# Four layers of cross attention on one core: layer 2's score products moved to the GELU, the first unit's odd maxima copied to f16 by ScalarE, the mask count cut in eight

## What is computed

```python
# layers 0, 1, 3 (with their own norms, biases and residuals)
scores = einsum('bhqd,bhkd->bhqk', q, k) * scale        # 16 heads, 100 x 1444
out    = einsum('bhqk,bhkd->bhqd', softmax(scores), v)
# layer 1 also has a mask of 100 x 1444 (all zero in the inputs)
# layer 2
sim    = softmax(where(causal, Q @ K.T / 8 ** 0.5, -1e9))
att_h  = layer_norm(sim @ V + q)
out    = gelu(att_h @ W1.T + b1, approximate=False) @ W2.T + b2 + att_h
```

## Time and profile before

| | us |
|---|---|
| median of three runs | 1051.69 |
| the profiled execution | 1052.03 |
| its span, first to last instruction | 1050.2 |
| stages -3 to -1 (ahead of the first exponential) | 76.7 |
| stages 0 to 5, each | 36.7 to 39.0 |
| stages 6 to 11, each | 35.1 to 35.4 |
| stage 12 (layer 2's attention alone) | 41.9 |
| stages 13 to 19 (attention and feed-forward), each | 50.4 to 53.1 |
| stage 20 (feed-forward alone) | 41.6 |
| stages 21, 22 | 34.6, 29.0 |

### The profile page before, as it was taken

One profiled execution on the slowest core, in us unless ns is written; L12 is line 12 of the kernel. 1 busy time (PEld: TensorE's weight loads), 2 busy tenths in 40 slices (PEclk: granted clock), 3 DMA queues, 4 the chain that ended last, 5 costly groups with the idle time before them and its releaser, 6 DMA issues.

```text
span 1050.2 us, 43883 instructions
## 1 busy us (share of the span) xinstructions
PE 947.4 (90%) x18826; PEld 570.9 (54%) x18826; DVE 839.8 (80%) x1804; ACT 717.6 (68%) x1621; POOL 372.3 (35%) x404
## 2 busy tenths in 40 slices
PE   1889999999989999999998979898979898989996
PEld 1346556656656665666564545555645464555552
DVE  7888988889788888889987777777878787869851
ACT  1147777777767777777776676667666676767786
POOL 3835345444323312332543434334343434212100
PEclk9669999999999999999999999999989898999999
DMA  8422313222232233233313121212121211212100
GB/s 225 110 62 72 83 50 88 78 69 60 78 95 69 89 95 104 66 93 96 96 52 86 35 82 38 68 38 69 43 62 44 69 51 61 71 36 66 52 4 6
DMA packets 63641, 73.75 MB, mean 70 GB/s; under 512 B 8130, under 2 KB 59114, under 8 KB 63318
## 3 DMA queue, kind: packets, MB, share of 16 engines
q1 hardware_dynamic: 63446, 70.92, 24.3%
HBM read 50.35 MB, written 18.15 MB: 65 GB/s over the span
## 4 chain that ended last, share of the span: by engine, by line
PE 66%; DVE 20%; ACT 5%; issue 4%; POOL 3%; DMA 1%; SPq 1%; POOLq 0%; ACTq 0%; DVEq 0%
PE ring L608 25%; PE sexp L608 15%; PE acc L778 15%; DVE mx L1246 7%; PE ring L651 6%; DVE mneg L1252 3%; DVE mx L1244 3%; POOL kbd L517 2%; ACT probs L1030 2%; PE ring L835 1%; PE ring L628 1%; DVE kp L1223 1%; PE ring L789 1%; DMA rows<-in_rows 1%; PE ring L734 1%
## 5 line engine op out<-in xcount | busy, mean ns | idle before, releaser
L1246 DVE TENSOR_TENSOR mx<-ring,mx 120x400 f16<-120x400 f32 (+1 forms) x1056 | 564.8, 566 | 114.6 <-PE ring L608 111.7
L1030 ACT ACTIVATE probs<-sexp 120x400 f32<-120x400 f32 (+1 forms) x1152 | 529.9, 509 | 139.2 <-PE sexp L608 134.6
L608 PE MATMUL ring<-qx,krep 96*32 96x400 f16 (+2 forms) x4608 | 418.2, 348 | 30.7 <-DVE mx L1246 8.1
L608 PE MATMUL sexp<-qx,krep 97*32 97x400 f16 (+2 forms) x4608 | 410.9, 340 | 8.4 <-ACT probs L1030 4.2
L778 PE MATMUL acc<-probs,vx 120*18 120x200 f32 (+1 forms) x4608 | 254.6, 336 | 1.0 <-ACT probs L1030 0.7
L608 PEld LDWEIGHTS ring<-qx,krep 96*32 96x32 f16 (+2 forms) x4608 | 133.8, 98 | 130.4 <-DVE mx L1246 42.7
L608 PEld LDWEIGHTS sexp<-qx,krep 97*32 97x32 f16 (+2 forms) x4608 | 133.4, 97 | 94.3 <-ACT probs L1030 28.4
L778 PEld LDWEIGHTS acc<-probs,vx 120*18 120x18 f32 (+1 forms) x4608 | 133.3, 99 | 65.9 <-issue 5.4
L534 POOL TENSOR_TENSOR qx<-qs,headmask 96x400 f16<-96x400 f16 x96 | 78.8, 849 | 150.0 <-DVE qs L1233 150.0
L497 POOL CAST ct<-ctf 128x480 f16<-128x480 f32 (+1 forms) x69 | 40.4, 585 | 135.1 <-PE ring L651 75.0
L608 PE MATMUL ring<-ct,wk 128*32 128x480 f16 (+1 forms) x864 | 65.4, 389 | 20.7 <-DVE mx L1246 20.0
(11 more groups left out here) (137 smaller groups left out, 865.0 us busy)
## 6 DMA issues: line engine op xcount, KB each, us to landing
krep<-kept SPq DMA_DIRECT2D x144, 120.0 KB, 2.8
...
```

Of the source, the lines that this page charges most:

```text
L608: last = run(out[g:g + m], w[:, g:g + m], x, **flags)
L1030: act.activation(probs[0:r, j % PR, :], sexp[j % SR][0:r, 0:QW], ACT.Exp).then_inc(sem["probs_ready"], 1)
L1246: op = dve.tensor_tensor(dst, src, dst, ALU.max)
```

## The change

The tables of steps move `xT` and `q` from steps 18 and 20 to 13 and 16, `k1` from 22 to 24 and `v0` to `v1`, `mk0` to `mk2`, `k2` by one step. Layer 2's scores move from 23, 25, 26, 28 to 20, 21, 22, 23; its exponentials from 29, 31, 32, 34 to 26, 27, 29, 30; the transposes from 32, 34, 35, 38 to 27, 29, 30, 32; `a`, `o` and `out` two steps ahead. Of the feed-forward part `scale` and `at` go one step back and `w2` from 27 to 34; `h` stays at 19. For unit 0 every second tile of the first pass is copied by ScalarE to `mcopy` in f16, and VectorE takes it from there. The count of the mask bytes is cut into eight pieces that stand in stage 0 at steps 4, 9, ... 39, with eight partial counts that are summed at the end.

```diff
-AT = {..., "xT": 18, "q": 20, "k1": 22, "v0": 24, ...
+AT = {..., "xT": 13, "wo": 15, "q": 16, "k1": 24, "v0": 25, ...
-AT2 = {"cx": 2, "kqv": 5, "s0": 23, "s1": 25, "s2": 26, "s3": 28, "e0": 29, "e1": 31, "e2": 32, "e3": 34,
+AT2 = {"cx": 2, "kqv": 5, "s0": 20, "s1": 21, "s2": 22, "s3": 23, "e0": 26, "e1": 27, "e2": 29, "e3": 30,
-AT2_FF = {"out": 0, "scale": 12, "at": 16, "h": 19, "w2": 27}
+AT2_FF = {"out": 0, "scale": 13, "at": 17, "h": 19, "w2": 34}
...
+        def copied_first(u, i):
+
+            return u is UNITS[0] and i % 2 == 1
...
             elif use[:4] == "smax":
-                pe.wait_ge(*at("smax_used", u, int(use[4:]) + 1))
+                i = int(use[4:])
+                if copied_first(u, i):
+                    pe.wait_ge(sem["m_copied"], i // 2 + 1)
+                else:
+                    pe.wait_ge(*at("smax_used", u, i + 1))
...
+            def maximum_copy(u, i):
+
+                r = chunk(i // T)[1]
+                act.wait_ge(*at("smax_used", u, i - 7))
+                act.wait_ge(*at("smax_ready", u, i + 1))
+                act.copy(mcopy[0:r, i // 2 % 4, :], bank(f"smax{i}", u)[0:r, 0:QW]).then_inc(sem["m_copied"], 1)
...
-                    if n == FLAG_STAGE - 1 and j == AT["v2"] + 1:
+                    if n == FLAG_STAGE and j % 5 == 4 and j < 40:
                         act.wait_ge(sem["mask_in_all"], 16)
-                        act.activation(anymask[:, :], anymask[:, :], ACT.Copy, accum_out=maskcount[:, :]
+                        piece = anymask[:, j // 5 * 1129:min(j // 5 * 1129 + 1129, B * S * KEYS // 128)]
+                        act.activation(piece, piece, ACT.Copy, accum_out=maskcount[:, j // 5:j // 5 + 1]
                                        ).then_inc(sem["mask_counted"], 1)
...
-                dve.wait_ge(*at("smax_ready", u, i + 1))
                 src, dst = bank(f"smax{i}", u)[0:r, 0:QW], mx[0:r, u.par, QW * t:QW * t + QW]
+                if u is UNITS[0] and c > 0:
+                    dve.wait_ge(*at("smax_used", u, i - T + 1))
+                if copied_first(u, i):
+                    dve.wait_ge(sem["m_copied"], i // 2 + 1)
+                    src = mcopy[0:r, i // 2 % 4, :]
+                else:
+                    dve.wait_ge(*at("smax_ready", u, i + 1))
```

More of the change, by code:

```diff
@@ L64 @@
 NSTEP = NCH * T
-AT = {"ct0": 0, "ct1": 3, "ct2": 6, "O": 7, "k0": 10, "OT": 12, "wo": 15, "xT": 18, "q": 20, "k1": 22, "v0": 24,
-      "mk0": 25, "v1": 27, "mk1": 28, "k2": 30, "mk2": 31, "v2": 33, "power": 25, "scale": 32, "mt0": 36, "mt1": 37, "mn": 41}
-AT2 = {"cx": 2, "kqv": 5, "s0": 23, "s1": 25, "s2": 26, "s3": 28, "e0": 29, "e1": 31, "e2": 32, "e3": 34,
-       "pt0": 32, "pt1": 34, "pt2": 35, "pt3": 38, "a": 42, "o": 44, "out": 45}
-AT2_FF = {"out": 0, "scale": 12, "at": 16, "h": 19, "w2": 27}
+AT = {"ct0": 0, "ct1": 3, "ct2": 6, "O": 7, "k0": 10, "OT": 12, "xT": 13, "wo": 15, "q": 16, "k1": 24, "v0": 25,
+      "mk0": 26, "v1": 28, "mk1": 29, "k2": 31, "mk2": 32, "v2": 33, "power": 25, "scale": 32, "mt0": 36, "mt1": 37, "mn": 41}
+AT2 = {"cx": 2, "kqv": 5, "s0": 20, "s1": 21, "s2": 22, "s3": 23, "e0": 26, "e1": 27, "e2": 29, "e3": 30,
+       "pt0": 27, "pt1": 29, "pt2": 30, "pt3": 32, "a": 40, "o": 42, "out": 43}
+AT2_FF = {"out": 0, "scale": 13, "at": 17, "h": 19, "w2": 34}
 HOLD = {"smax": 1.6, "k": 3.0, "v": 2.0, "ct": 2.0, "O": 2.8, "q": 2.6, "xT": 1.6, "mt": 2.6, "mn": 1.6, "OT": 1.8,
@@ L131, in build @@
         anymask = sb("anymask", [128, B * S * KEYS // 128], U8)
-        maskcount = sb("maskcount", [128, 1])
+        maskcount = sb("maskcount", [128, 8])
+        masksum = sb("masksum", [1, 9])
         maskflag = sb("maskflag", [1, 1], I32)
@@ L156, in build @@
         mx = sb("mx", [128, 2, T * QW], F16)
+        mcopy = sb("mcopy", [128, 4, QW], F16)
         mneg = sb("mneg", [S, H], F16)
@@ L205, in build @@
             "mask_ready": [0, 3, 0, 0], "maskexp_in": [0, 32, 0, 0],
-            "smax_ready": STEPS, "smax_used": STEPS, "mt_filled": [2, 2, 0, 2],
+            "m_copied": [0, 0, 0, 0], "smax_ready": STEPS, "smax_used": STEPS, "mt_filled": [2, 2, 0, 2],
             "m_ready": [2, 2, 0, 2], "mn_filled": one, "mrow_ready": one, "mrow_in": [16, 16, 0, 16],
@@ L227, in build @@
         setup_names = ["ident_in", "wk_in", "x_in", "const_in", "wq_ready", "wv_ready", "pool_ready", "ones_ready", "acc_zero", "wk_ready", "x_ready", "rest_ready", "x_power", "x_root", "setup",
-                       "mask_in_all", "mask_counted", "flag_filled", "flag_ready"]
+                       "mask_in_all", "mask_counted", "flag_filled", "flag_summed", "flag_ready"]
         sem = {name: es.enter_context(nc.semaphore(name)) for name in list(PER) + setup_names}
@@ L904, in flag_sum @@
             def flag_sum():
-                pe.wait_ge(sem["mask_counted"], 1)
+                pe.wait_ge(sem["mask_counted"], 8)
                 ps = begin("flag", None)
-                pe.matmul(ps[0:1, 0:1], maskcount[:, :], ones[:, :], start=True, stop=True
+                pe.matmul(ps[0:1, 0:8], ones[:, :], maskcount[:, :], start=True, stop=True
                           ).then_inc(sem["flag_filled"], 1)
@@ L1080, in stage @@
                 for j in range(NSTEP):
+                    m = max_tile(s, j)
+                    if m is not None and copied_first(*m):
+                        maximum_copy(*m)
                     if s.exp is not None:
@@ L1108, in stage @@
                         act.wait_ge(sem["flag_filled"], 1)
-                        act.copy(maskflag[:, :], bank("flag", None)[0:1, 0:1]).then_inc(sem["flag_ready"], 1)
+                        act.activation(masksum[:, 0:8], bank("flag", None)[0:1, 0:8], ACT.Copy, accum_out=masksum[:, 8:9]
+                                       ).then_inc(sem["flag_summed"], 1)
+                        act.wait_ge(sem["flag_summed"], 1)
+                        act.copy(maskflag[:, :], masksum[:, 8:9]).then_inc(sem["flag_ready"], 1)
             act.wait_ge(sem["pool_ready"], 1)
```

## The result

The changed kernel takes 1046.80 us (median of 10 runs, 1042.54 to 1049.96), the kernel before 1053.39 beside it (10 runs, 1050.79 to 1056.97): ratio 0.9936, 95% interval 0.9918 to 0.9954. The forecast was 1025, its range 1010 to 1042. The direction is right, the gain is 6.6 us where 26.8 were summed up. The profiled execution took 1046.76 us, with a span of 1045.0.

What follows compares the result with a forecast made beforehand. TensorE, busy 90% of the span, was taken as the bound, with idle time and slow clock in stages 13 to 19. Gains 23.8 + 1.0 + 2.6 + 1.9 - 2.5 = 26.8 us took 1052.0 to 1025 us, range 1010 to 1042.

Steps and rivals of the forecast that it cites:

- Stages 13 to 16: Part of layer 2's stages 13 to 19, forecast to gain 3.4 us a stage, 23.8 us in seven.
- The hole: 3.64 us in stage 14 without exponentials on ScalarE, from the GELU table load to the end of the second load.
- the 18.0 us up to step 34: Stage 14, first table load to the exponential of step 34: forecast 18.0 us in place of 21.7.
- The other stages: Stages bound by TensorE's unchanged work, with moved keys, query and values: 0 us (-2 to +1 in all).
- stage 12: Scores but no hole; VectorE gets eight operations in five steps: 0 us (-1 to +1).
- The first pass: Unit 0's opening: 24 of 48 maxima read f16 copies in SBUF, at 0.35 us each; gain 2.6 us (0 to 4).
- The mask: Mask count cut up: 1.9 us come off ahead of stage 0, eight pieces in stage 0 cost 2.5 us (0 to 5).
- Stage 20: It has the hole but no score products to fill it: gain 1.0 us (0 to 1.5).
- Rival 1: Consecutive scores fill the ring, VectorE falls behind, TensorE waits for `sc`: gain 1.5 a stage, 1038.5 us; chance 0.21.
- rival 2: TensorE idles so little that its clock stays at 2.4 GHz: about 1.4 us more a stage, 1015 us; chance 0.13.
- rival 3: Transposes closer behind their exponentials block TensorE, each costing some 1 us, four a stage: slower, 1058 us; chance 0.06.
- Rival 4: Query still stops VectorE, at step 16, opening is TensorE's; only mask and half the hole won: 1042 us; chance 0.07.

Runs made afterwards that it cites:

- e15_after_y: The changed kernel with the residual add of layer 3's stages and its centring four steps later: 1035.10 us, ratio to before 0.9845.

## Why the prediction was wrong

**Stages 13 to 16: right.** 3.4 us a stage forecast, 13.0 / 4 = 3.2 measured. The hole, its place, `qs` and the 18.0 us up to step 34 came out as written. That the stage's sum agrees too is in part luck: from a stage's start to step 34 the four give 4.1 us each, more than forecast (3.7 in stages 14 and 16, more in 13 and 15, where before's trace has a second slow stretch), and behind step 34 they lose 0.9 each, of which the forecast knew nothing. The sum stopped at step 34, and took the exchange of `w2` for two transposes as "about the same work on TensorE". That step failed: with `w2` at 27 the same stages give (205.7 - 187.2) / 4 = 4.6. On VectorE, which I did not count for it, `w2` brings 0.28 us ahead of two reductions of 1.15 and 1.00 between them, and 0.7 of that only because GpSimd's subtraction runs at that place. A sum was wrong too, with little weight: VectorE's terms for steps 20 to 25 (6 x 0.5, 8 x 0.56 and one `kp` of 0.7) make 8.2 us, not 8.7.

**Stages 17 to 19: the step that carried stage 14's 3.4 us over to all seven failed.** They have another unit behind them (layer 3's) and an add of 2.45 us at step 11. With it behind the `kbd` products they give (153.8 - 137.4) / 3 = 5.5 us each, not 1.2. Of the difference 1.5 us a stage are the add's own; the other 8 us in three stages are four slow stretches, two each in stages 17 and 19, that the changed kernel's trace has and that of `e15_after_y` has not. I had read stage 17's length, not its rows.

**The other stages: "0 (-2 to +1 in all)" and stage 12 "0 (-1 to +1)" failed.** 9.6 of the 12.4 us that they lose are shown to be the tables' (5.8 in stages 7 to 11, 3.8 in stage 12): I took them as TensorE's (34.5 busy of 35.3 us) and so immune to an order that leaves its work alone. But TensorE's waits of 0.3 to 0.6 us in stages 7 to 11 of the changed kernel are for VectorE, which was busy 31.8 of the 35.3 us itself and got 0.9 us more from stage 9 on.

**The first pass: the mechanism failed.** 2.6 us for copies that make VectorE's operation 0.35: it is 0.35 where GpSimd is idle or runs a memset or `rinv`, and up to 1.57 beside its products, and GpSimd was busy 24.7 of 33.4 us, which stood in my own row. **The mask:** -1.9 and +2.5 forecast; -1.9 and +3.4 in its own trace, but only 1.6 to 2.3 of the latter are the count's; no measurable time in all: right in kind. **Stage 20:** 1.0 forecast, 1.9 measured.

**The rivals.** None names what happened. Rival 1's wait (TensorE for `sc`) is what layer 2's tables make without the query, and in the changed kernel it stands in stage 12 (0.47 and 0.50 us), where the forecast had nothing; rival 2's full clock comes in some stages (15) and not in others (14, 17); rival 3's transposes hold TensorE up for 0.71 us once in stage 12 and once in 13, and in no stage from 14 to 19 by over 0.2. Rival 4's 1042 is nearest in time and false in its reason: where VectorE waits longest for `qh` at 16 (1.89 us in stage 17), behind a slow stretch, no wait of TensorE ends with it. The range left out the sum of several small losses outside the place of the change.

What stays open: which wait in the opening makes the copies a loss and not a draw, how the 3.8 us of stage 12 divide among the three moves, and what decides whether a slow stretch follows a wait.
